# Steps of the first stage put off by ten, zeros written first, and another signal that paces the scatters

## The reference, cut to what matters

```
xt = layernorm(x)                       # T = 16384 tokens
top1 = argmax(softmax(xt @ w_router))   # 32 experts
pos = running count of tokens per expert, in token order
slot = top1 * 640 + pos, if pos < 640, else dropped
buf[slot] = xt                          # 20480 rows, unused ones zero
```

## Time and profile before

| | |
|---|---|
| median of three runs | 1685.2 us |
| the profiled execution's own time | 1685.51 us |
| its span, first to last instruction | 1683.7 us |
| first scatter starts | 91.13 us |
| last scatter of the first stage starts | 301.99 us |
| SP reads the first expert's rows | 304.75 us |
| PE, DVE, ACT, Pool busy in the span | 83%, 70%, 69%, 45% |

### The profile page before, as it was taken

How to read it: one execution, slowest core, us unless ns; L and a number is a source line. 1 busy time by engine, 2 the same in 40 slices (tenths; PEclk the granted TensorE clock), 3 DMA queues, 4 the chain that set the end, 5 groups by cost and what they waited for, 6 DMA issues and landing times. The chain is left out here.

```text
span 1683.7 us, 33159 instructions
## 1 busy us (share of the span) xinstructions
PE 1402.5 (83%) x10920; PEld 1311.8 (78%) x10920; DVE 1178.0 (70%) x3207; ACT 1165.5 (69%) x2458; POOL 761.4 (45%) x989
## 2 busy tenths in 40 slices
PE   4345550699999999789999999999745999999997
PEld 3223330599999999679999999999635999999997
DVE  5255552477778787568788888878654878787875
ACT  7567770477777777468887878877545777777774
POOL 0045556234343434334457666666542343434343
PEclk7555655799999999889999999999867999999999
DMA  9977753466666666430222322221104444444441
GB/s 367 370 224 248 255 171 110 161 204 233 226 206 216 234 221 194 150 127 14 76 76 69 99 90 69 78 66 44 55 26 146 124 121 139 144 139 122 147 142 39
DMA packets 196889, 250.12 MB, mean 149 GB/s; under 512 B 24650, under 2 KB 182008, under 8 KB 192624
## 3 DMA queue, kind: packets, MB, share of 16 engines
q1 hardware_dynamic: 169072, 204.23, 37.8%
q0 software_dynamic: 27648, 43.78, 7.5%
HBM read 128.05 MB, written 152.17 MB: 166 GB/s over the span
## 5 line engine op out<-in xcount | busy, mean ns | idle before, releaser
L955 PE MATMUL ps<-xs,ws 128*128 128x320 f32 x3072 | 466.3, 311 | 4.6 <-DVE hf L909 4.5
L955 PEld LDWEIGHTS ps<-xs,ws 128*128 128x128 f32 x3072 | 455.8, 189 | 5.7 <-issue 5.7
L343 POOL DMA_INDIRECT slots<-xn,r x256 | 257.0, 1004 | 253.8 <-issue 172.1
L955 PE MATMUL ps<-ws,hs 128*128 128x256 f32 x1920 | 261.9, 288 | 10.7 <-DVE ys L894 8.7
L782 POOL DMA_INDIRECT x_rows<-ys,oidx x160 | 155.9, 975 | 251.1 <-DVE ys L894 173.2
L782 POOL DMA_INDIRECT out<-ys,oidx x160 | 155.9, 975 | 250.7 <-DVE ys L894 173.3
L955 PEld LDWEIGHTS ps<-ws,hs 128*128 128x128 f32 x1920 | 239.0, 190 | 23.9 <-issue 21.9
L909 DVE TENSOR_TENSOR hf<-ps,sg 128x320 f32<-128x320 f32 x256 | 125.9, 492 | 145.1 <-issue 99.7
L411 PE MATMUL ps<-cf,xn 128*128 128x128 f32 x512 | 102.6, 334 | 106.0 <-ACT xn L365 72.5
L803 ACT CAST xs<-ps 128x512 fp32r<-128x512 f32 (+1 forms) x192 | 98.6, 514 | 130.8 <-PE ps L948 130.8
L365 ACT ACTIVATE xn<-x,r 128x256 f32<-128x256 f32 x256 | 138.8, 591 | 55.7 <-DVE r L318 33.0
(11 more groups left out here) (119 smaller groups left out, 2482.3 us busy)
## 6 DMA issues: line engine op xcount, KB each, us to landing
slots<-zero SPq DMA_DIRECT2D x32, 1300.0 KB, 18.5
xg<-slots SPq DMA_DIRECT2D x62, 650.0 KB
x<-in_x SPq DMA_DIRECT2D x32, 512.0 KB, 5.0
x_rows<-x SPq DMA_DIRECT2D x32, 512.0 KB
wraw<-in_w_gate SPq DMA_DIRECT2D x64, 256.0 KB
wraw<-in_w_up SPq DMA_DIRECT2D x64, 256.0 KB
wraw<-in_w_down SPq DMA_DIRECT2D x64, 256.0 KB
x<-x_rows SPq DMA_DIRECT2D x32, 512.0 KB, 6.1
```

What stands on the lines that cost most here:

```text
L343: nc.gpsimd.indirect_dma_start(out=self.slots, out_offset=bass.IndirectOffsetOnAxis(ap=self.slot[:, t % self.xr, k:k + 1], axis=0), in_=se ...
L955: ins = pe.matmul(dst, left(a, k), right(b, k), start=(n == 0), stop=(n == len(terms) - 1))
```

## The change

Zeros: all 16 blocks are issued before the first store; quarters 6 to 11 stand one after each of blocks 0, 2, 3, 5, 6 and 8. Stores and loads: after the store of quarter q comes the load of quarter q+10 instead of q+12 ahead of it, so that two stores lie between a store and the load that waits for it. Steps: each engine's work on pairs 24 and up is put off by ten steps (`place`, GAP); the distances within the work on one pair or one choice are the same as before (POST and SCATTER are counted from the last pair of a choice now, which gives the same step). Pool: pair p waits until ACT has copied pair p+17 (from pair 46 on: pair 63), and of two choices in one step the earlier one is scattered first.

```diff
-                POST, SCATTER, BASE = 15, 20, 3
+                POST, SCATTER, BASE = 8, 13, 3
+                GAP = 10
+                def place(n):
+                    return n if n < 3 * NC else n + GAP
+                def put(S, lag):
+                    return [n for n in (S - lag, S - lag - GAP) if 0 <= n < NU and place(n) + lag == S]
+                def chosen(S, lag):
+                    return [c for c, (t, lo, hi) in enumerate(CHOICES) if place(NC * t + hi // CH - 1) + lag == S]
...
-                    nf = 0
-                    for q in range(6, 4 * XR):
-                        for n in range(nf, nf + 2 - q % 2):
-                            fill(sp, 0, slots1, n)
-                        nf += 2 - q % 2
-                        stream.load(sp, q)
-                    fill(sp, 0, slots1, nf)
-                    stream.store(sp, 0, tail.based)
-                    for n in range(nf + 1, NFILL):
+                    for n in range(NFILL):
                         fill(sp, 0, slots1, n)
+                        if n % 3 != 1 and 6 + n * 2 // 3 < 4 * XR:
+                            stream.load(sp, 6 + n * 2 // 3)
                     for q in range(NQ4):
-                        if q:
-                            stream.store(sp, q, tail.based)
-                        if q + 4 * XR < NQ4:
-                            stream.load(sp, q + 4 * XR)
+                        stream.store(sp, q, tail.based)
+                        if q >= 2 and q - 2 + 4 * XR < NQ4:
+                            stream.load(sp, q - 2 + 4 * XR)
...
-                    for S in range(SCATTER, NU + SCATTER):
-                        if S <= NU:
-                            pool.wait_ge(tail.normed.sem, tail.normed.at(S))
-                        for u in range(NC):
-                            for c in choices(S, SCATTER + u):
-                                if 2 * u < CHOICES[c][2] - CHOICES[c][1]:
+                    for S in range(SCATTER, NU + GAP + SCATTER + NC):
+                        for u in reversed(range(NC)):
+                            for c in chosen(S, SCATTER + u):
+                                t, lo, hi = CHOICES[c]
+                                if 2 * u < hi - lo:
+                                    p = NC * t + lo // CH + u
+                                    pool.wait_ge(tail.evac.sem, tail.evac.at(min(p + 18, NU)))
                                     tail.pool_scatter(pool, c, u)
```

In the programs of ACT, DVE and PE each test on S becomes the same test on `place`, `put` or `chosen`, for example:

```diff
-                        if 0 <= S < NU:
-                            tail.act_norm(act, S)
+                        for n in put(S, 0):
+                            tail.act_norm(act, n)
...
-                            if lo - lead[g] == S:
+                            if place(lo) - lead[g] == S:
```

More of the change, by code:

```diff
@@ L635, in _ @@
                     nc.scalar.preload_act_table_set("natural_log_exp_and_others")
-                    for S in range(-2, NU + 22):
+                    for S in range(-2, NU + GAP + 22):
                         for g, (lo, hi) in enumerate(groups):
-                            if max(lo - 3, lo - lead[g] + 1) == S:
+                            if place(lo) + max(-3, 1 - lead[g]) == S:
                                 tail.act_rstd(act, g)
-                        for c in choices(S, POST + 2):
+                        for c in chosen(S, POST + 2):
                             tail.act_exp(act, c)
-                        if 0 <= S < NU:
-                            tail.act_norm(act, S)
[L644 to L649, removed]
+                        for n in put(S, 0):
+                            tail.act_norm(act, n)
+                        for n in put(S, 2):
+                            tail.act_evac(act, n)
+                        for n in put(S, 6):
+                            if n % 2 == 0:
+                                tail.act_keep(act, n // 2)
+                        for n in put(S, BASE):
+                            tail.act_base(act, n)
                 @block.vector
@@ L654, in _ @@
                     tail.rdone.grant(dve)
-                    for S in range(-2, NU + 22):
+                    for S in range(-2, NU + GAP + 22):
                         for q in (3, 2, 1, 0):
-                            for c in [c for c in range(len(CHOICES)) if c in choices(S, POST + PARTS[c][q])]:
+                            for c in [c for c in range(len(CHOICES)) if c in chosen(S, POST + PARTS[c][q])]:
                                 tail.post(dve, c, q)
                         for g, (lo, hi) in enumerate(groups):
-                            if max(lo - 1, lo - lead[g] + 2) == S:
+                            if place(lo) + max(-1, 2 - lead[g]) == S:
                                 tail.dve_factors(dve, g)
                         for g, (lo, hi) in enumerate(groups):
-                            if lo - lead[g] == S:
+                            if place(lo) - lead[g] == S:
                                 for n in range(lo, hi):
@@ L688, in _ @@
                     tail.pe_setup(pe)
-                    for S in range(NU + 22):
+                    for S in range(NU + GAP + 22):
                         if S == 4:
@@ L696, in _ @@
                             ins.then_inc(s_prep, 1)
-                        for c in choices(S, POST + 2):
+                        for c in chosen(S, POST + 2):
                             tail.pe_count(pe, c)
[L699 to L704, removed]
+                        for n in put(S, 0):
+                            tail.pe_turn(pe, n)
+                        for n in put(S, 4):
+                            if n % 2 == 0:
+                                tail.pe_raw(pe, n // 2)
+                        for n in put(S, 7):
+                            if n % 2 == 0:
+                                tail.pe_logits(pe, n // 2)
                     tail.pe_total(pe)
```

## The result

The changed kernel takes 1673.52 us, the median of six runs (1670.38 to 1674.61), against 1684.43 us for the kernel before (six runs, 1683.01 to 1690.73): a ratio of 0.9925, 95% interval 0.9907 to 0.9944. The medians lie 10.9 us apart, which is 0.65%; the ratio says 0.75%. The forecast was 1672.8. In the profiled executions (1672.02 us after, span 1670.2) SP reads the first expert's rows at 293.77 instead of 304.75: 11.0 us of the gain are there. The time from that read to the end of the span is 1378.9 before and 1376.4 after (1683.7 - 304.75, 1670.2 - 293.77); these 2.5 us lie in stages that the change does not touch.

A forecast was written before the change was run, and what follows sets the result against it. The first stage's last scatter was taken as the bound, with PE's signals held while Pool scatters. Terms 111 + 39 x 3.0 + 5.6 + 56.7 = 290.3 against 302.97, 12.7 us earlier, gave 1672.8 us; range 1651 to 1689.

The forecast's parts named there:

- First scatter 77, run of 14 to 94.9: Pool's first scatter comes near 77 us instead of 91.13, and 14 scatters run unbroken to 94.9.
- Signals held until 96.5, norm 24 at 111: PE's signals wait out Pool's first run; 14.2 us of DVE's work follow, putting pair 24's norm near 111, against 101.04.
- Pace 3.0: Each of 39 pairs after pair 24's norm takes 3.0 us, between ACT's 2.73 and 3.5.
- The part on Pool's wait: Pool, waiting for ACT's copy, stops a pair later when signals are held; lost time per hold falls from 6 to 2 or 3 us.
- Copy 63 at +5.6: ACT's copy of pair 63 follows its norm by 5.6 us: 7.8 less a hold of 2.2.
- Tail 56.7 with a gap of 6.6 before choice 8: Pool's last scatters after copy 63: 28.7 us, a 6.6 us gap for choice 8's slots, then 21.4.
- Sum: First stage's last scatter: 111 + 39 x 3.0 + 5.6 + 56.7 = 290.3 against 302.97, 12.7 us earlier.
- Loads at nothing: SP's loads two stores behind were priced at nothing but 3.5 us on quarter 12, hidden by DVE's later step.
- Ten steps later and zeros first: Zeros end near 75.9 us, choice 0's slots no longer wait behind quarter 12; ACT does pairs 20 to 23 at once.
- B: Rival: the pace stays 3.35 us a pair as Pool's runs stay unbroken; 304.0, 1686.5 us; chance 0.17.
- C: Rival: Pool's scatters, PE's signal and ACT's copy wait in a loop, 3.5 to 3.9 us a pair, slower from 3.33; chance 0.12.
- A: Rival: Pool's first run holds nothing that counts; 98.5 + 39 x 2.9 + 62.3 = 273.9, 29 us gained, 1656.4; chance 0.2.

The follow-up runs named there:

- e4: The changed kernel with the load of quarter q+12 right behind the store of quarter q, one store between instead of two: 1675.06 us, ratio 0.9950 to the kernel before.
- e1: The changed kernel without the ten steps' delay of pairs 24 and up (GAP 0): 1669.31 us, ratio 0.9923 to the kernel before.
- e3: The changed kernel with the zeros, first store and quarters 6 to 11 ordered as before: 1666.89 us, ratio 0.9905 to the kernel before.
- e2: The changed kernel with Pool's pair p waiting for the norm of pair p+19 again, as before: 1673.8 us, ratio 0.9946 to the kernel before.
- e11: The changed kernel with Pool paused after six scatters until PE's logits up to pair 23, on a chip that holds signals: 1668.62 us, ratio 0.9887.
- e10: The changed kernel with Pool paused after six scatters until PE's logits up to pair 23, on a chip that holds no signals: 1616.67 us, ratio 0.9894.
- e9: The changed kernel itself, unedited, on a chip that holds no signals: 1618.26 us against 1634.48 for the kernel before, ratio 0.9902.

## Why the prediction was right, step by step

- **First scatter 77, run of 14 to 94.9:** 77.13 and 94.90. Quarter 12 "about 82": the statistics that need it were no longer on the path.
- **Signals held until 96.5, norm 24 at 111:** the hold is real (97.39) but norm 24 came at 105.76. The sum queued all of DVE's 14.2 us behind the end of the run. PE's count of choice 1 got through at 89.45, in the middle of it, so part 3 and one group of statistics were done in the shadow of the hold, and only 8.4 us of work lay between the copy at 97.39 and the norm. A hold ends signal by signal (89.36, 90.78 and 97.36 by the signals' own records), not all at the end of the run. The prediction had both ends; it took the outer one.
- **Pace 3.0:** 3.13. The part on Pool's wait said that the lost time would fall from 6 us per batch to 2 or 3. Each hold did (at most 2.8 us of ACT's idle time instead of 6.0), but they came about twice in a batch, and ACT's idle time ahead of its copies stayed at 18.3 us against 19.4. Term by term, 39 x 0.13 = 5.2 us too little, which makes up for the 5.2 too much at norm 24: norm 63 was forecast at 228 and came at 227.93. That hit is two misses that cancel.
- **Copy 63 at +5.6:** +8.75 (end 236.68). A hold of 3.68 us stood before copy 62. Without it the term is 5.07, half a microsecond from the forecast, which had taken the hold of 2.22 out and put none in its place; 3.1 us too little.
- **Tail 56.7 with a gap of 6.6 before choice 8:** 55.4 (236.68 to 292.05). The gap (6.34) came before the last four scatters, not before choice 8: before, PE's count of choice 8 reached DVE only at 278.43, after the run of 24; now it arrives at 251.14, 7.5 us late but in the midst of the run of 34, and Pool goes on without a stop until the last choice, whose slots are late (286.4).
- **Sum:** 290.3 forecast, 292.05 measured, 1.75 us too early; the later stages gave 2.5 us back.
- **Loads at nothing:** wrong as a price of the edit, and it did not show because the forecast's pace never asked for it. The prediction had the number in its own rows: a load each 5.9 us is 2.95 us a pair, hardly under its 3.0. With one store between, e4's loads take 6.45 and bound the pace at 3.23 up to pair 44. The "ten steps ahead" held only for a pace set elsewhere.
- **Ten steps later and zeros first:** they move the first scatter as forecast; e1 and e3 show that this start is worth nothing. That holds beside the new wait and the new loads; e2 shows that without the new wait an earlier norm 25 carries 7.7 us of stage end. The prediction's sum gives the whole gain to the pace (norm 24 moves back by 10). Measured, 3.9 us of what looks like pace is work of ACT's that the ten steps let it do ahead, and how the rest divides between wait, loads and steps is not settled by taking out one part at a time.
- **Rivals:** B (pace unchanged) fell with 3.13, C (a loop) with Pool's runs of two and six by turns, 14 at the start and 34 at the end; its condition of 3.33 was nearly met by e2 and e4, at 3.32 and 3.28, which still gained 0.5%, since their norm 24 came 4.5 to 10 us before the 111 on which that condition rests. A, the first run that holds nothing, is what happens on the other kind of chip: norm 24 at 98.57 as its sum has it (98.5), pace 2.64, just below the floor of 2.73, and a gain of 16.2 us, 1.0%. Its price, 29 us, was made against a kernel before that is itself held; where nothing is held that kernel is faster too. What the prediction could not know is that A and the forecast are both true, each on its chips.

## What to carry to other kernels

An engine that starts earlier may gain nothing when the stage ends by the pace of the one behind it (e1): take the sum from pace times count first, and look in the trace for every resource that is near that pace (here, for a pace of 3.0, loads at 2.95 us a pair, ACT at 2.73, Pool at 2.56). Measure both paces from a place that lies behind the same holds, or a hold that has only moved counts as a gain. When parts are taken out one at a time and sum to nothing, test them in pairs before giving any its price. When Pool issues indirect DMAs in a long run, look for idle time put down to "remote" on other engines; if it is there, a wait in Pool's program on the signal that is being held can cut the hold short (97.39 to 86.22 in e11), and it cost nothing that could be told where there is none (e10 beside e9). The label alone proves nothing: look whether the arrival of the signal is on record. Compare versions only on one chip: the chip alone moved this kernel by 3%, the change by 0.75 to 1.0%.

## What was not expected of the hardware

The late signals went with the chip: 46 of 79 recorded PE signals late on one, none of 86 on another, for the same program. A run of scatters does not hold every signal to its end: in the run of 34 the count of choice 8 got through at 251.14, the first row below. And on the first chip DVE's own steps are late too, near the end of that run: from the end of DVE's reduction at 275.05 (L490) to its next one 5.60 us pass with no releaser but "remote", beside Pool's scatters:

```profile
251.16 0.42 DVE L497 TENSOR_TENSOR r<-r,ps 128x256 f32<-128x256 bf16 x1 [7.47 <-remote]
...
274.77 0.28 DVE L490 TENSOR_REDUCE r<-r 128x4 f32<-128x128 f32 x1
280.65 0.25 DVE L492 TENSOR_SCALAR xn<-r 128x4 f32<-128x4 f32 x1 [5.60 <-remote]
```

And the run that did it drew little: from 235 to 285 us the DMA share was 0.40 at 136 GB/s.
